# Opening of an LRU, attention and MoE kernel: loads split by first use, states in halves, kept rows on ScalarE, logits in their own groups

## The reference

```python
Bu = einsum('blh,nh->bln', u, B_re + 1j*B_im) * gamma      # 64 complex states
x_n = Lam * x_(n-1) + Bu_n                                 # a linear scan over the 1024 rows
y = einsum('bln,on->blo', x, C).real + u @ D.T
# the FFN part, itself with a residual each:
h = x + attention(rmsnorm(x, ln1))      # 16 heads of 8, softmax over 1024 keys
h = h + moe(rmsnorm(h, ln2))            # 8 experts, the two with the highest logits
```

## Time and profile before

| | |
|---|---|
| median of 3 runs | 1005.19 us (1004.36 to 1005.29) |
| the profiled execution | 1006.17 us, of which its span is 1004.4 us |
| TensorE busy | 872.2 us, 87% of the span |
| VectorE busy | 854.3 us, 85% |
| ScalarE busy | 696.9 us, 69% |
| GpSimd busy | 403.0 us, 40% |
| chain that ended last | TensorE 58%, VectorE 26%, ScalarE 8%, issue 5% |
| mean granted TensorE clock | 0.963 of full speed (0.5 of it is 1.2 GHz, 1 is 2.4 GHz) |
| most time on the chain | values weighed (L1670) 21%, row maxima (L1225) 13%, column scores (L1660) 9% |

### The profile page before, as it was taken

One profiled execution on the slowest core, in us unless ns is written; L12 is line 12 of the kernel. 1 busy time (PEld: TensorE's weight loads), 2 busy tenths in 40 slices (PEclk: granted clock), 3 DMA queues, 4 the chain that ended last, 5 costly groups with the idle time before them and its releaser, 6 DMA issues.

```text
span 1004.4 us, 18298 instructions
## 1 busy us (share of the span) xinstructions
PE 872.2 (87%) x5968; PEld 364.4 (36%) x5968; DVE 854.3 (85%) x1451; ACT 696.9 (69%) x1487; POOL 403.0 (40%) x621
## 2 busy tenths in 40 slices
PE   0378888999999999999999999999999999889990
PEld 0256641222222223222222222222322246688990
DVE  4978889999999998988989898898799966667663
ACT  2735233888888887888888888888788876545660
POOL 7234540011010153433705534363687403336774
PEclk9879996999999999999999999999999999999995
DMA  9997642011000110100101010010101011122346
GB/s 313 387 355 201 185 120 61 9 26 32 9 25 9 33 25 9 46 10 25 54 9 25 12 44 19 24 46 10 25 31 42 24 43 47 43 63 67 105 147 198
DMA packets 60829, 74.34 MB, mean 74 GB/s; under 512 B 9152, under 2 KB 39104, under 8 KB 60352
## 3 DMA queue, kind: packets, MB, share of 16 engines
q1 hardware_dynamic: 53936, 62.93, 21.4%
q0 software_dynamic: 4608, 9.58, 2.8%
q10 hardware_dynamic: 2192, 0.66, 0.3%
HBM read 28.09 MB, written 44.79 MB: 73 GB/s over the span
## 4 chain that ended last, share of the span: by engine, by line
PE 58%; DVE 26%; ACT 8%; issue 5%; ACTq 1%; POOL 1%; DMA 1%; POOLq 0%; DVEq 0%; SPq 0%
PE ps L1670 21%; DVE nmax L1225 13%; PE ps L1660 9%; PE ps L1546 8%; ACT prob L981 7%; PE ps L1772 7%; PE ps L1788 3%; PE ps L1535 2%; PE ps L1733 2%; PE ps L1565 1%; DVE wk L1173 1%; POOL by_token L813 1%; ACTq L839 1%; PE ps L1693 1%; PE ps L1752 1%
## 5 line engine op out<-in xcount | busy, mean ns | idle before, releaser
L1225 DVE TENSOR_REDUCE nmax<-ps 128x1 f32<-128x1024 f32 x512 | 602.1, 1220 | 43.8 <-PE ps L1546 39.5
L981 ACT ACTIVATE prob<-ps 128x512 f32<-128x512 f32 x1024 | 529.7, 603 | 90.5 <-PE ps L1660 88.7
L1546 PE MATMUL ps<-packs 50*128 50x512 bf16 x1024 | 342.8, 389 | 9.5 <-DVE nmax L1225 5.4
L1660 PE MATMUL ps<-packs 50*128 50x512 bf16 x1024 | 312.3, 384 | 30.1 <-ACT prob L981 20.8
L1670 PE MATMUL ps<-prob,vpad 128*32 128x512 f32 x2048 | 273.6, 606 | 0.0
L1546 PEld LDWEIGHTS ps<-packs 50*128 50x128 bf16 x1024 | 74.8, 94 | 239.7 <-DVE nmax L1225 184.8
L1660 PEld LDWEIGHTS ps<-packs 50*128 50x128 bf16 x1024 | 75.9, 94 | 144.9 <-ACT prob L981 94.2
L547 POOL MEMSET packs<- 2x2048 bf16 x32 | 57.5, 1796 | 171.1 <-PE ps L1660 169.9
L813 POOL DMA_INDIRECT by_token<-wk,vall x80 | 79.8, 997 | 97.9 <-DVE wk L1315 61.4
L1772 PE MATMUL ps<-ws 128*128 128x128 f32 x640 | 88.5, 282 | 3.2 <-DVE ws L1335 2.4
L1772 PEld LDWEIGHTS ps<-ws 128*128 128x128 f32 x640 | 79.8, 196 | 9.0 <-issue 7.4
(11 more groups left out here) (307 smaller groups left out, 873.2 us busy)
## 6 DMA issues: line engine op xcount, KB each, us to landing
by_expert_rows<-prob SPq DMA_DIRECT2D x4, 5016.0 KB, 36.9
packs<-k_parts SPq DMA_DIRECT2D x32, 192.0 KB, 3.6
packs<-q_parts SPq DMA_DIRECT2D x64, 96.0 KB, 3.1
vall<-by_expert_rows SPq DMA_DIRECT2D x80, 66.0 KB
packs<-by_token SPq DMA_DIRECT2D x8, 512.0 KB, 5.1
w<-w_t SPq DMA_DIRECT2D x3, 1024.0 KB, 10.9
q_parts<-front SPq DMA_DIRECT2D x16, 192.0 KB, 3.2
k_parts<-front SPq DMA_DIRECT2D x16, 192.0 KB, 3.2
```

The costliest lines, as they stand in the source:

```text
L981: act.activation(prob[:, v % RING, :], bank(col_bank(pos)), ACT.Exp).then_inc(col_free, 1)
L1225: dve.tensor_reduce(nmax[:, half, par, pair, qt:qt + 1], bank(first, 2), AX_X, ALU.max, negate=True).then_inc(row_free, 1)
L1546: ins = pe.matmul(bank(first + kh), qpack[r:r + ROWS, slot, half, pair, qt * P:(qt + 1) * P], kpack[r:r + ROWS, slot, pair, kh * HALF:(kh ...
L1660: pe.matmul(bank(col_bank(pos)), kpack[r:r + ROWS, slot, head // 2, kt * P:(kt + 1) * P], qpack[r:r + ROWS, slot, half, head // 2, :], sta ...
```

## The change

Six edits.

1. ScalarE keeps five loads: `nu` and `th` on `angle_in`, `gam` and the two of `wB` on a new semaphore `wb_in`. The other twelve go to SyncE, behind x and ahead of the fills, on `w_in`. The expert weights move behind the fills. Exp on `gam` now comes before the Sin functions.
2. z of batches 0 to 2 is computed by ScalarE, by eight activations with scale and bias behind the high parts of the batch; z of batch 3 stays on GpSimd. VectorE computes the biases (`off_za`), one small operation more for each of the three batches, on the new semaphore `z_offset`.
3. In `states` the addition and the scan run in two halves; the second scan starts from the last column of the first.
4. TensorE makes 22 unused products between turn_u(1) and product_y(0), in bank 6, after the first two multiplications of the states of batch 0 (`bu_read`).
5. `logits` of blocks 0 to 3 move from group 5 to group 4, `prefix` from 9 to 8.
6. The product of L1704 is gone.

```diff
-        FRONT_AT = {t: ((2 * t + 4, 7), (2 * t + 4, 9), (2 * t + 5, 3), (2 * t + 5, 5), (2 * t + 5, 9), (2 * t + 5, 9))
+        FRONT_AT = {t: ((2 * t + 4, 7), (2 * t + 4, 9), (2 * t + 5, 3), (2 * t + 5, 4), (2 * t + 5, 8), (2 * t + 5, 9))
                     for t in range(4)}
...
@@ block.sync
-            for dst, src in ((w13[:, 0], w1_t), (w13[:, 1], w3_t), (w2[:, :], w2_t)):
-                sp.dma_start(dst, src).then_inc(wl_in, 16)
+            for dst, src in ((wC[0:NS, 0, :], c_re_t), (wC[NS:P, 0, :], c_im_t),
+                             (wC[0:NS, 1, :], c_im_t), (wC[NS:P, 1, :], c_re_t),
+                             (wD[:, :], d_t), (ln1c[:, :], ln1), (ln2c[:, :], ln2), (wq[:, :], wq_t), (wk[:, :], wk_t),
+                             (wv[:, :], wv_t), (wo[:, :], wo_t), (wgate[:, :], gate_t)):
+                sp.dma_start(dst, src).then_inc(w_in, 16)
...
+            for dst, src in ((w13[:, 0], w1_t), (w13[:, 1], w3_t), (w2[:, :], w2_t)):
+                sp.dma_start(dst, src).then_inc(wl_in, 16)
...
@@ block.gpsimd
-            for b in range(B):
-                keep_z(b, b)
+            for b in range(B - 1):
                 lower_parts(b)
+            keep_z(B - 1, 0)
+            lower_parts(B - 1)
...
@@ block.scalar
+            for dst, src in ((nu[:, :], nu2), (th[:, :], theta2)):
                 act.dma_start(dst, src).then_inc(angle_in, 16)
-            for dst, src in loads[2:]:
-                act.dma_start(dst, src).then_inc(w_in, 16)
+            for dst, src in ((gam[:, :], gamma_row.to_broadcast([P, P])), (wB[:, 0, :], b_pack), (wB[:, 1, :], b_swap)):
+                act.dma_start(dst, src).then_inc(wb_in, 16)
             act.wait_ge(angle_in, 16 * 2)
...
+            act.wait_ge(wb_in, 16 * 3)
+            act.activation(gam[:, :], gam[:, :], ACT.Exp).then_inc(lam_ready, 1)
...
+            def keep_z(b):
+
+                act.wait_ge(z_offset, b + 1)
+                for t in range(b * TILES, (b + 1) * TILES):
+                    j = t % TILES
+                    ins = act.activation(zres[:, t, :], xacc[:, t, :], ACT.Identity, bias=off_za[:, b % 2, 0, j:j + 1],
+                                         scale=roots[:, b % 2, 2 * TILES + j:2 * TILES + j + 1])
+                ins.then_inc(z_kept, 1)
...
+                if not last:
+                    keep_z(b)
                 if b + 3 < B:
                     norm_u(b + 3)
...
@@ block.vector
-                step(dve.tensor_tensor(bu_back, bu_back, state_back, ALU.add))
-                step(dve.tensor_tensor_scan(state_back, lam[:, 0:1].to_broadcast([P, L]), bu_back, 0.0, ALU.mult, ALU.add))
                 for half in range(2):
                     c = slice(half * HALF, (half + 1) * HALF)
+                    step(dve.tensor_tensor(bu_back[:, c], bu_back[:, c], state_back[:, c], ALU.add))
+                    step(dve.tensor_tensor_scan(state_back[:, c], lam[:, 0:1].to_broadcast([P, HALF]), bu_back[:, c],
+                                                state_back[:, HALF - 1:HALF] if half else 0.0, ALU.mult, ALU.add))
...
+                if b + 1 < B:
+                    dve.scalar_tensor_tensor(off_za[:, b % 2, 0, :], stats[:, :, 0], -1.0, y[:, 0:TILES],
+                                             ALU.mult, ALU.mult).then_inc(z_offset, 1)
...
@@ block.tensor
             turn_u(1)
+            pe.wait_ge(pads, 1)
+            pe.wait_ge(bu_read, 1)
+            unused_products(22, to=6)
             product_y(0)
...
                 elif name == "logits":
-                    if not late:
-                        pe.matmul(out[:, HALF // 2:HALF], ident[:, :], flat13[:, 0:HALF // 2],
-                                  start=True, stop=True, skip_group_check=True)
```

More of the change, by code:

```diff
@@ L126, in build_program @@
         u_T = (u_even, sb("u_odd", [P, L])[:, :])
-        off_a = sb("off_a", [P, 2, 4])
+        off_za = sb("off_za", [P, 2, 2, TILES])
         bu_back, state_back, x_cos, x_sin = (wk4[:, i, :] for i in range(4))
@@ L203, in build_program @@
         x_in = [sem("x_in%d" % b) for b in range(B)]
[L204 removed]
+        angle_in, wb_in, w_in, wl_in = sem("angle_in"), sem("wb_in"), sem("w_in"), sem("wl_in")
         rest_ready = sem("rest_ready")
@@ L219, in build_program @@
         u_ready, z_ready, z_kept, a_ready = sem("u_ready"), sem("z_ready"), sem("z_kept"), sem("a_ready")
+        z_offset = sem("z_offset")
         hi_ready = sem("hi_ready")
@@ L581, in keep_z @@
                           roots[:, b % 2, 2 * TILES:3 * TILES].unsqueeze(2), n, z_kept, 1)
+                gp.wait_ge(z_kept, B)
             def lower_parts(b):
@@ L828, in _ @@
         def _(act):
-            loads = [(nu[:, :], nu2), (th[:, :], theta2), (gam[:, :], gamma_row.to_broadcast([P, P])),
-                     (wB[:, 0, :], b_pack), (wB[:, 1, :], b_swap),
-                     (wC[0:NS, 0, :], c_re_t), (wC[NS:P, 0, :], c_im_t),
-                     (wC[0:NS, 1, :], c_im_t), (wC[NS:P, 1, :], c_re_t),
-                     (wD[:, :], d_t), (ln1c[:, :], ln1), (ln2c[:, :], ln2), (wq[:, :], wq_t), (wk[:, :], wk_t),
-                     (wv[:, :], wv_t), (wo[:, :], wo_t), (wgate[:, :], gate_t)]
-            for dst, src in loads[:2]:
+            for dst, src in ((nu[:, :], nu2), (th[:, :], theta2)):
                 act.dma_start(dst, src).then_inc(angle_in, 16)
-            for dst, src in loads[2:]:
-                act.dma_start(dst, src).then_inc(w_in, 16)
+            for dst, src in ((gam[:, :], gamma_row.to_broadcast([P, P])), (wB[:, 0, :], b_pack), (wB[:, 1, :], b_swap)):
+                act.dma_start(dst, src).then_inc(wb_in, 16)
             act.wait_ge(angle_in, 16 * 2)
@@ L850, in _ @@
                            bias=trig[:, 15:16]).then_inc(sin_ready, 1)
-            act.wait_ge(w_in, 16 * 15)
-            act.activation(gam[:, :], gam[:, :], ACT.Exp).then_inc(lam_ready, 1)
+            act.wait_ge(w_in, 16 * 12)
             act.mul(wC[NS:P, 0, :], wC[NS:P, 0, :], -1.0).then_inc(b_scaled, 1)
@@ L1504, in _, with unused_products @@
             pe.wait_ge(consts, 13)
-            pe.wait_ge(w_in, 16 * 15)
+            pe.wait_ge(w_in, 16 * 12)
             pe.wait_ge(b_scaled, 4)
+            def unused_products(n, to=0):
+                for _ in range(n):
+                    pe.matmul(ps[:, to, 0:2 * P], ident16[:, :], ident[:, :].bitcast(BF16), start=True, stop=True)
             def turn_u(b):
@@ L1596, in batch @@
                     pe.wait_ge(v_saved, b + 1)
-            def unused_products(n):
-                for _ in range(n):
-                    pe.matmul(ps[:, 0, 0:2 * P], ident16[:, :], ident[:, :].bitcast(BF16), start=True, stop=True)
             def last_half(b):
```

7 lines of the change are left out of this document (3 added, 4 removed).

## The result

The changed kernel takes 999.68 us at the median of five executions (996.56 to 1000.06), the kernel before 1005.19 us beside it (1004.36 to 1005.61). The ratio is 0.9933, with a 95% interval of 0.9918 to 0.9948: 5.5 us faster, where 10.1 were forecast. The time lies in the stated range (987 to 1001) and in the bracket of rival 2 (998 to 1002), outside the forecast's own band (992 to 998). The profiled execution took 999.88 us, its span is 998.1 us against 1004.4, so 6.3 us are to be found in the two traces. Five executions are few, and they lie in two groups, 996.6 and 999.7 to 1000.1. The profile shows one of the upper group.

What follows compares the result with a forecast made beforehand. The prediction took a serial opening chain of waits across engines, then the attention loop, to bound the kernel. Loads -1.85, batches -4.5 and logits -3.8 sum to -10.1: 995.1 us at the median, forecast 992 to 998, range 987 to 1001.

Steps and rivals of the forecast that it cites:

- rival 2: Opening: new waits eat the gain, GpSimd keeping its port or the clock falling in every new gap; 998 to 1002, chance 0.15.
- Loads and U: Opening: earlier loads move the end of VectorE's first chain (U, 44.70 us, start of the batches) by -1.85 us.
- the sum: Whole kernel: opening loads -1.85, batches -4.5 and logits -3.8 us, together -10.1.
- Rival 1: Opening: GpSimd's narrow memsets hold no VectorE operation, 5.65 us more gain, median 989.4; 987 to 992, chance 0.20.
- Batches: Opening's four batches: state halves, rows kept by ScalarE and filler together give -4.5 us, between -8 and -2.
- the walk: Opening's batches: instants forecast step by step after VectorE's first chain, last rows at 81.3 instead of 85.8 us.
- the projections warm: TensorE's projections in batch 0: at full clock they end near 25 instead of 31.9 us after VectorE's first chain.
- Halves: VectorE's addition and scan in `states`: split in two, the first pair of products is ready 1.75 us earlier.
- z on ScalarE: Batches 1 to 3: with `keep_z` off GpSimd the scan falls from 3.87 to 2.29 us, 1.58 less.
- Logits: Attention loop: removed product and logits in groups of their own, six items on TensorE's chain, -3.8 us.
- Rival 4: Attention loop: slower, as without the removed product TensorE's clock could fall in the quads; 1015 with six falls, chance 0.04.

Runs made afterwards that it cites:

- the base: The changed kernel itself, run again beside the follow-up kernels: 1049.89 us, ratio 0.9925 to the kernel before.
- three edits: Changed kernel with opening memsets as float32, `keep_z` behind `norm_u`, and the Exp table loaded in ScalarE's idle time: 995.86 us, ratio 0.9908 to the kernel before.

## Why the prediction was right, and where not

**Loads and U: right in mechanism and nearly in size.** -2.30 against -1.85. Exp on `th` started at 5.42, not 6.85. x landed at 8.9 instead of 8.0 at the latest, so the statistics began at 8.99 and not 8.3: rows 2 give a median of three loads, and the one that the statistics wait for took 7.59 us from its issue at 1.30. Three operations of VectorE waited for one memset each, as the sum had it by the two-partition memsets holding VectorE in turns, and L1136 was hardly held. The rule of the Trainium skill that was weighed there ("SBUF — State Buffer", section "SBUF: two separate sides") is borne out for a memset on two partitions: with the memsets early the operations took 0.17 us. Rival 1's condition is refuted, though a kernel without the hold has U 4.5 us earlier and would, by the trace with float32 memsets, have had its first cast no earlier (149.73 against 149.80); rival 1 left out that other engines give it back.

**Batches: -2.42 instead of -4.5, the step that was most mis-sized.** By the walk's own instants, in us after U: states(1) at 19.27 (forecast 19.3), projections done at 26.05 (25), `turn_u(3)` at 35.05 (35), states(2) at 42.56 (41.4), last rows at 83.38 (81.3). So the walk held up to `turn_u(3)`, its wait and its cause included. Then the fall of the clock was worth more: the turn and `product_bu(2)` took 1.97 and 5.5 instead of 1.09 and 3.60, 2.8 us more where some 2 were forecast, and states(2) were 1.2 us later than forecast. L1215 was held for 1.25 us at 100.41, which the forecast had at 0.4, and TensorE idled again ahead of `turn_a(2)`, with projections of 6.56: 0.9 us more. The run with `keep_z` behind `norm_u(3)` speaks for the first: without that idle time the last rows come 2.3 us earlier than in the base. Against a scatter of 2.9 us in one program's last rows this is a tendency; what is shown by itself is each link, the wait for ScalarE, the clock at 0.50 behind it, and VectorE's wait of 2.81 for the slow products. The forecast took "the projections warm" from the first batch and did not carry the same question, does TensorE idle ahead of it, to each later batch.

**Halves: not shown to give anything.** The sum had 1.75 us of it and pushed the first product by 1 us for the filler. The filler ended at 49.63, 7.2 us after U, so the halves' first products at U + 5.8 waited for it in full. If the pair of edits gives something in batch 0, it is the filler's, about 2 us.

**z on ScalarE: 0 to 2 us.** The scans are indeed at 1.28, and the 1.58 us each that the forecast counted are real, but ScalarE's 3.2 us delay `turn_u(3)`. "SyncE's writes of the parts are shorter than the shortened batch: nothing" was true in this trace and false one step on: as soon as the opening became shorter, the stores were what it waited for (4.41 us with float32 memsets, 6.28 with three edits). The expert weights behind the fills, also put at nothing, had a part in it, since with them the first stores took 10.4 us to land instead of 3.4. The prediction had named as its root that neither ScalarE nor SyncE sets the batches' pace. The batches did shorten, by about half of what was forecast, ScalarE set the instant of `turn_u(3)`, and SyncE's stores set that of the high parts once U or ScalarE's rows came earlier.

**The loop's start: missed.** +1.54 us. The prediction costed the order of loads on ScalarE and not the order of its functions. 1.05 us are the table load; 0.3 to 0.5 a longer stretch at half the clock.

**Logits: -2.6 instead of -3.8.** The four half-quads of blocks 0 to 3 gave 0.56 to 0.59 each, 2.3 in all, against 0.63. Blocks 4 and 5 were counted like them. The half-quads around them went from 25.22 to 24.79, 22.64 to 22.24 and 20.80 to 21.25: -0.4 in all instead of -1.3.

**Rivals.** The time fell into rival 2's bracket, in part by its mechanism. Of its two conditions the clock's came near, with falls in new idle stretches and batches that gave 2.42, where it had 2. The other didn't come, for GpSimd didn't keep its port, and U gave 2.30. The moved loads cost nothing that a trace shows; x itself landed 0.9 us later than forecast. The rest is the loop's start, which no rival had. So the forecast's sum was nearly twice the gain, and that the time lies in the stated range is owed to the range's upper end. Rival 4's point was tested by the changed kernel itself: no fall of the clock from 175 to 890 us. Summed with what was measured, -2.30 - 2.42 + 1.54 - 2.59 - 0.5 = -6.3.

## What to carry to other kernels

Read ScalarE's order of functions as a resource: which table stood when the loop started was decided by the last exponential or sine before it, and one dummy function in idle time put the load there. When an opening is shortened, walk every queue that hands over to the loop, the stores' too, for a gain upstream is only kept if the stage that is late next has slack; here moving SyncE's stores and the weights' loads was worth 3.2 us once the waits ahead of it had gone. Ask of a large load moved in a queue whose landings it will delay, not only when it is wanted itself. And ahead of each block of products ask anew whether TensorE idles, since a warm first batch says nothing of the next.

## What the runs showed of the hardware

- A memset of GpSimd on two partitions (1.84 us) holds a VectorE operation on 16 values of 128 partitions as one on 128 partitions does; written as float32 the same bytes take 0.98 us (3.93 for four) instead of 1.84 (7.35 for four).
- VectorE's operations and GpSimd's memsets took turns: one operation of VectorE ended with each memset, three in a row (14.70, 16.56 and 18.41 us).
- The same instruction stream had its later states up to 2.9 us apart between executions, with the granted clock rising and falling at other instants each time (first rise in the filler or behind it at 47.7 in one, 50.7 in another), while U agreed to 0.03 us.
- SyncE's issue of four fills of 5 MB took 33.5 us of its own time (15.16 to 48.65), and the three weight loads behind them 16.0. In the kernel with three edits the four stores issued right behind those took 12.3 us to land at the median, against 6.3 without the weight loads ahead of them and 3.4 in the kernel before.
